# A two-layer decoder on one core: the opening of the first attention reordered, batch by batch, and the expert weights loaded in pieces

## The chip, the cores and the metric

One core of one Trainium2 chip runs the kernel. The metric is the device time of one execution in microseconds (us): the median of three timed runs, 528.86 before the change. A profile of one further execution goes with it.

## What is computed

Two decoder layers on x of 4 batches x 256 tokens x 128 features, all in float32, each with self attention, cross attention and a mixture of experts, always added to x after a layer norm. What the change touches is the first sublayer and the preparation of the second:

```python
q, k = rope(xn @ wq.T), rope(xn @ wk.T)        # 16 heads of 8 features
out  = softmax(q k^T / sqrt(8)) @ (xn @ wv.T)  # no mask, per batch of 256 tokens
# second sublayer, from the context alone:
K, V = ctx @ Wk.T, ctx @ Wv.T
ek   = exp(K - max over the 4 batches)         # keys
ep   = exp(W_bias - W_bias)                    # the maximum runs over an axis of length 1
num, den = ep @ (ek * V), ep @ ek
# third sublayer, 8 linear experts: each w_in[e] is multiplied with w_out[e] once
```

The rotated q and k are used as a rounded part and its rest (float32r, the one-pass matmul type), so that two one-pass products stand for one four-pass product.

## The kernel before, in words

The order of the work on each engine is written out by hand: one program per engine, which waits on named semaphores. Each engine runs its instructions in order, so a wait holds all that stands behind it. The 1024 tokens are 8 tiles of 128; a batch is 2 tiles, a half is 2 batches.

*Loads.* SP's queue (L259 to L287) issues 28 loads, x first, the 2 MB `wi0` and the 2 MB `wo0` of the experts last. ScalarE's queue (L461 to L463) issues the context `ctxT`, its weights `wctx`, then `ident`, the identity for transposes.

*Opening, TensorE* (L1160 to L1177): `context` (L1144), tiles 0 to 3, each giving keys and values of the second sublayer and values of the fifth, in banks 4 and 5 in turn, released by ScalarE's three copies (L475 to L477); `transpose_xn` of both halves (L1141); `rotary_projections(0)`, four 512-column products (q, k, and each with neighbours swapped; L1158); values of both halves (L1172); `context` tiles 4 to 7; `rotary_projections(1)`, each after VectorE's rotation has read the bank.

*Opening, the others.* VectorE: norm statistics, normalising, the rounding of the selection matrices `selr` (L752), the rotations of half 0 and the products of half 1 (`rotate`, L760, 512 wide), sums (L767) and rests (L772) of half 0, then the context's maximum over batches (L786 to L788). GpSimd: memsets (L323 to L335, three of them for later layers), `rstds` (L337), the sums of half 1 (L356), the context's differences (L360), the bias's difference (L364), the rests of half 1 (L368), then `head_values` (L344), which lays the values of four heads into `vaug`. ScalarE: copies, the rounded parts (L501), and the exponentials of context keys and bias (L516, L518).

*Attention* (`attention` on each engine, `pipelined`, L239): 4 batches of 16 slots plus a drain; slot k of batch b begins head k of batch b. The operands of a batch are *stacked* first: with `selr`, four heads' q and k (rounded part, rest) are put into one 128-row block `qk`, 32 rows per head. `first_stacks` (L1187) does this for batch 0, ScalarE copies the four groups out (L482); later batches are stacked inside the slots (`KEY_SLOTS`, `QUERY_SLOTS`) through bank 6. SP copies each head's 32 key rows into the zeroed `km` (`padded_keys`, L289 to L301: 4 copies of 32 KB per group of four heads). In slot k, `max_scores` (L1215) computes the scores whose row maxima VectorE takes (L823); in batch 0 it uses the stacked keys for groups 0 and 1 and `km` for 2 and 3. Every four heads the maxima are transposed into `qk` (L1259, L830). Seven slots later `exp_scores` (L1233) computes the scores again, with `km` and the maxima, and ScalarE takes the exponential (L541). Twelve slots after a group began come its values (L1262). The banks: 0 and 1 maxima, 2 and 3 exponentials, 4 values, 5 transposes, 6 stacks, 7 output rows.

The exponentials of the context are used by `aft_sums` (L1324) in the drain and after it. The expert weights are used at L1358, after the second sublayer.

Of the kernel before, what the change touches and what calls it, by code (L numbers as in the profile page):

```python
# [12 lines left out]
P = 128  # L13
# [10 lines left out]
FIRST_BANKS = (6, 7, 4, 5)  # L24
LN_EPS, Z_EPS = 1e-5, 1e-6
# [29 lines left out]
def decoder_kernel(nc, w, out):  # L55
# [4 lines left out]
    with ctx:  # L60
# [57 lines left out]
        ek = sb_early("ek", [P, TPB, B, D])  # L118
        ekv = sb_early("ekv", [P, TPB, B, D])
        v_tok = sb_early("v_tok", [P, NT, D])  # L120
        early.close()
# [22 lines left out]

# [3 lines left out]
        ctx_max = big[:, 6144:6912].rearrange("p (m k d) -> p m k d", m=3, k=TPB)  # L148
# [108 lines left out]
        def _(sp):  # L257
# [7 lines left out]
            load("xa0", wx0[:, :, :], w["wx0"])  # L265
            load("xa0", wbiasT[:, :, :], w["wbiasT"])
            load("gate0", wgate0[:, :], w["wgate0"])
            load("gate0", tie0[:, :, :], w["tie0"].partition_broadcast(P))
# [17 lines left out]
            load("ff0", wi0[:, :, :, :], w["wi0"])  # L286
            load("ff0", wo0[:, :, :, :], w["wo0"])  # L287

            def padded_keys(L):  # L289

                for n in range(B * G):
# [28 lines left out]
        def _(pool):  # L320
# [14 lines left out]
            pool.memset(first_row[0:1, :], 1.0).then_inc(s("at1_row"), 1)  # L335
# [15 lines left out]
            for hf in range(2):  # L351
                rstds("at0", hf)

            for n, a in enumerate((1, 0)):
                pool.wait_ge(s("at0_rot"), 4 + 2 * (n + 1))
                pool.tensor_tensor(rot1[1][:, a, :], rot1[1][:, a, :], rot2[1][:, a, :], ALU.add).then_inc(s("at0_sum1"), 1)  # L356

            pool.wait_ge(s("ctx_mx"), 1)
            for k in range(TPB):
                pool.tensor_tensor(ek[:, k, :, :], ek[:, k, :, :],  # L360
                                   ctx_max[:, 2, k:k + 1, :].broadcast_to([P, B, D]), ALU.subtract).then_inc(s("ctx_kd"), 1)

            pool.wait_ge(s("ld_xa0"), 32)
            pool.tensor_tensor(expbT[:, :, :], wbiasT[:, :, :], wbiasT[:, :, :], ALU.subtract).then_inc(s("ctx_kd"), 1)  # L364

            for n, a in enumerate((1, 0)):
                pool.wait_ge(s("at0_hi"), 2 + n + 1)
                pool.tensor_tensor(qlo[:, a, HALF:2 * HALF], rot1[1][:, a, :], qhi[:, a, HALF:2 * HALF].bitcast(f32),  # L368
                                   ALU.subtract).then_inc(s("at0_lo1"), 1)
            pool.wait_ge(s("at0_vev"), 2)  # L370
# [5 lines left out]
            pool.tensor_tensor(ekv[:, :, :, :], ek[:, :, :, :], ekv[:, :, :, :], ALU.mult).then_inc(s("ctx_ekv"), 1)  # L376
# [77 lines left out]
        def _(act):  # L454
# [6 lines left out]
            for name, dst, src in (("ctx", ctxT[:, :], "ctxT"), ("ctx", wctx[:, :, :], "wctx"),  # L461
                                   ("ident", ident[:, :], "ident")):
# [7 lines left out]
            def context(tiles):  # L470

                for n in tiles:
                    b, jt = n // TPB, n % TPB
                    act.wait_ge(s("ctx_pe"), n + 1)
                    act.activation(ek[:, jt, b, :], ps[:, 4 + n % 2, 0:D], ACT.Copy)  # L475
                    act.activation(ekv[:, jt, b, :], ps[:, 4 + n % 2, D:2 * D], ACT.Copy)
                    act.activation(v1_tok[:, n, :], ps[:, 4 + n % 2, 2 * D:3 * D], ACT.Copy).then_inc(s("ctx_ev"), 1)  # L477
# [19 lines left out]
            def rotated(hf):  # L497

                for n, a in enumerate((1, 0)):
                    act.wait_ge(s(("at0_sum", "at0_sum1")[hf]), n + 1)  # L500
                    act.activation(qhi[:, a, hf * HALF:hf * HALF + HALF], rot1[hf][:, a, :], ACT.Copy  # L501
                                   ).then_inc(s("at0_hi"), 1)

            context(range(NT // 2))
            for hf in range(2):
                evacuate_xnT("at0", hf)
            for hf in range(2):
                act.wait_ge(s("at0_v"), hf + 1)
                act.activation(v_tok[:, 4 * hf:4 * hf + 4, :], ps[:, 6 + hf, :].rearrange("p (n d) -> p n d", d=D),
                               ACT.Copy).then_inc(s("at0_vev"), 1)  # L510
            rotated(0)
            context(range(NT // 2, NT))
# [1183 lines left out]
```

## Time and profile before

| | |
|---|---|
| runs shown | 527.92, 528.86, 533.05 us; median 528.86 |
| profiled execution | 533.33 us, its span 531.6 us |
| mean granted TensorE clock | 0.931 of 2.4 GHz |
| busy: TensorE, VectorE, ScalarE, GpSimd | 87%, 66%, 61%, 25% of the span |
| the chain that ended last | TensorE 64%, VectorE 15%, "issue" 9%, ScalarE 6%, GpSimd 3%, DMA 2% |
| DMA | 16.07 MB, mean 30 GB/s; 8.82 MB of it in the first 30 us |

The chain is followed back from the last instruction: at each step to what released it. Shares are averages over stages with different limits. The first scores begin at 32.3 us. TensorE's busy time counts pipelined matmuls with modelled ends. Names in the rows: `bigr<-qk` on SP's queue are the padded keys, `nmax` VectorE's row maxima.

### The profile page before, as it was taken

The page shows a single profiled execution, that of the slowest core. Times are in us where ns is not written, and L with a number is a line of the kernel's source. Part 1 is how long each engine was busy: PE and PEld are TensorE (multiplying, and loading weights), DVE is VectorE, ACT ScalarE, POOL GpSimd, SP SyncE. Part 2 cuts the span into 40 slices and gives each one's busy share as a digit, 9 for nine tenths or more (in the row PEclk, how much of TensorE's full clock was granted, in tenths as well). Part 3 has the DMA queues.
Part 4 walks back from the last instruction along what each step waited for, and adds up shares of the span by engine and source line. Part 5 has one row for each costly group of instructions (what it writes and reads, how often), then busy time and mean ns, then how long its engine had stood idle before and what let it go on. Part 6 is the DMA issues. An engine that isn't in the chain of part 4 may idle for free.

```text
span 531.6 us, 8533 instructions
## 1 busy us (share of the span) xinstructions
PE 463.6 (87%) x2692; PEld 356.8 (67%) x2692; DVE 351.8 (66%) x967; ACT 324.8 (61%) x632; POOL 133.0 (25%) x195
## 2 busy tenths in 40 slices
PE   3777999988993998579999867999999999999995
PEld 2446777755831686448777745878778787878783
DVE  4375677767589565546778845858585767777653
ACT  2444767642255442035665527898988989898892
POOL 7060000212165100114545420121112221111121
PEclk9976999998998898857999977999999999999999
DMA  8911111000300000001111000000000000000001
GB/s 296 368 25 31 31 32 28 19 1 1 159 1 0 1 1 1 0 21 40 32 31 28 14 0 1 1 2 0 1 0 0 0 0 0 0 0 1 2 0 39
DMA packets 12754, 16.07 MB, mean 30 GB/s; under 512 B 4008, under 2 KB 11304, under 8 KB 12080
## 3 DMA queue, kind: packets, MB, share of 16 engines
q1 hardware_dynamic: 12288, 14.79, 8.8%
q10 hardware_dynamic: 432, 0.85, 0.4%
q8 instruction: 18, 0.29, 0.2%
q14 instruction: 16, 0.13, 0.1%
HBM read 10.92 MB, written 0.52 MB: 22 GB/s over the span
## 4 chain that ended last, share of the span: by engine, by line
PE 64%; DVE 15%; issue 9%; ACT 6%; POOL 3%; DMA 2%; SPq 1%; ACTq 0%; POOLq 0%; DVEq 0%
PE ps L1229 6%; PE ps L1274 4%; PE ps L1544 4%; PE ps L1545 4%; PE ps L1543 4%; PE ps L1562 4%; PE ps L1561 4%; PE ps L1560 4%; PE ps L1241 3%; POOL xnT L447 2%; DVE masked L816 2%; PE ps L1551 2%; PE ps L1462 2%; PE ps L1149 2%; DVE big L933 1%
## 5 line engine op out<-in xcount | busy, mean ns | idle before, releaser
L1078 DVE TENSOR_TENSOR bigr<-ps,bigr 128x512 fp32r<-128x512 f32 x128 | 86.3, 689 | 57.8 <-ACT ps L681 57.8
L541 ACT ACTIVATE big<-ps 128x512 f32<-128x512 f32 (+1 forms) x128 | 68.7, 548 | 52.9 <-PE ps L1241 50.9
L680 ACT ACTIVATE bigr<-ps,b 128x512 fp32r<-128x512 f32 x128 | 89.8, 702 | 3.6 <-PE ps L1545 0.7
L681 ACT ACTIVATE ps<-ps,b 128x512 f32<-128x512 f32 x128 | 86.6, 677 | 0.0
L447 POOL TENSOR_TENSOR xnT<-xnT,big 128x512 f32<-128x512 f32 x32 | 41.4, 1293 | 162.4 <-DVE big L1085 162.4
L1229 PE MATMUL ps<-bigr,qk 128*128 128x256 f32 (+1 forms) x224 | 53.8, 323 | 5.4 <-DMA bigr<-qk 2.8
L823 DVE TENSOR_REDUCE nmax<-ps 128x2 f32<-128x512 f32 x64 | 42.6, 688 | 18.8 <-PE ps L1229 18.4
L1241 PE MATMUL ps<-qk,bigr 128*128 128x256 f32 (+1 forms) x256 | 51.2, 284 | 1.0 <-ACT big L541 0.7
L1543 PE MATMUL ps<-k1hi,w1hi 128*128 128x512 f32 x128 | 51.5, 402 | 0.0
L1544 PE MATMUL ps<-k1hi,w1lo 128*128 128x512 f32 x128 | 51.3, 401 | 0.0
L1545 PE MATMUL ps<-k1lo,w1hi 128*128 128x512 f32 x128 | 51.2, 400 | 0.0
L1560 PE MATMUL ps<-bigr,w2hi 128*128 128x512 f32 x128 | 51.0, 398 | 0.0
L1562 PE MATMUL ps<-bigr,w2hi 128*128 128x512 f32 x128 | 50.7, 396 | 0.0
L1561 PE MATMUL ps<-bigr,w2lo 128*128 128x512 f32 x128 | 50.4, 394 | 0.0
L816 DVE CUSTOM_DVE_ANT_0 masked<-ps,later 128x128 f32<-128x128 f32 (+1 forms) x128 | 39.0, 352 | 16.2 <-PE ps L1229 15.8
L1229 PEld LDWEIGHTS ps<-bigr,qk 128*128 128x128 f32 x224 | 35.7, 200 | 14.6 <-issue 5.7
L1241 PEld LDWEIGHTS ps<-qk,bigr 128*128 128x128 f32 x256 | 41.2, 199 | 3.7 <-ACT big L541 2.3
L424 POOL TENSOR_SCALAR_AFFINE_SELECT big<-big 128x256 f32<-128x256 f32 x64 | 26.0, 411 | 46.5 <-ACT big L541 46.2
L1274 PE MATMUL ps<-big,vaug 128*32 128x256 f32 (+1 forms) x512 | 30.9, 358 | 2.2 <-POOL big L424 1.3
L672 ACT ACTIVATE big<-ps 128x512 f32<-128x512 f32 x32 | 19.2, 599 | 20.7 <-PE ps L1551 20.6
L1544 PEld LDWEIGHTS ps<-k1hi,w1lo 128*128 128x128 f32 x128 | 24.6, 192 | 6.0
L1545 PEld LDWEIGHTS ps<-k1lo,w1hi 128*128 128x128 f32 x128 | 24.5, 191 | 5.9
(200 smaller groups left out, 864.3 us busy)
## 6 DMA issues: line engine op xcount, KB each, us to landing
bigr<-qk SPq DMA_DIRECT2D x128, 32.0 KB, 1.9
wi<-in_wi SPq DMA_DIRECT2D x1, 2048.0 KB, 7.6
wo<-in_wo SPq DMA_DIRECT2D x1, 2048.0 KB, 12.1
big<-in_sel SPq DMA_DIRECT2D x1, 1024.0 KB, 8.6
wo<-in_w SPq DMA_DIRECT2D x1, 1024.0 KB, 4.8
wi<-in_w SPq DMA_DIRECT2D x1, 1024.0 KB, 6.9
x<-in_x SPq DMA_DIRECT2D x1, 512.0 KB, 5.5
ctxT<-in_ctxT ACTq DMA_DIRECT2D x1, 512.0 KB, 4.9
```

What stands on the lines that cost most here:

```text
L541: act.activation(prob[:, h % 8, c], ps[:, 2 + h % 2, c], ACT.Exp, scale=DH ** -0.5).then_inc(s(L + "_exp"), 1)
L680: act.activation(ghi[:, u % 2, c, :], ps[:, c, :], ACT.Gelu_apprx_tanh, bias=b1[:, u % E1, c:c + 1])
L681: act.activation(ps[:, c, :], ps[:, c, :], ACT.Gelu_apprx_tanh, bias=b1[:, u % E1, c:c + 1]).then_inc(s("ff1_gel"), 1)
L1078: v.tensor_tensor(glo[:, u % 2, c, :], ps[:, c, :], ghi[:, u % 2, c, :].bitcast(f32), ALU.subtract).then_inc(s("ff1_glo"), 1)
L1229: last = pe.matmul(ps[:, h % 2, at:at + seen], qk[rows, g, 0, t * P:t * P + P], keys[:, 0:seen], start=True, stop=True)
L1241: last = pe.matmul(ps[:, 2 + h % 2, at + first:at + T], km[:, h, t * P:t * P + P], qk[:, h // HPG, 0, first:T], start=True, stop=True)
L1543: pe.matmul(ps[:, k, :], w1hi[:, e, f], xhi[:, c], start=True, stop=False)
L1544: pe.matmul(ps[:, k, :], w1lo[:, e, f], xhi[:, c], start=False, stop=False)
L1545: pe.matmul(ps[:, k, :], w1hi[:, e, f], xlo[:, c], start=False, stop=True).then_inc(s("ff1_up"), 1)
L1560: pe.matmul(o, w2hi[:, e, k, :], ghi[:, u % 2, k, :], start=(k == 0), stop=False)
L1561: pe.matmul(o, w2lo[:, e, k, :], ghi[:, u % 2, k, :], start=False, stop=False)
L1562: last = pe.matmul(o, w2hi[:, e, k, :], glo[:, u % 2, k, :], start=False, stop=(k == FC - 1))
```

## The change

- *ScalarE's loads*: `ident` first, then `ctxT`, `wctx`.
- *TensorE ahead of the first stack*: context tiles 0 and 1, transposes of half 0, context tile 2, the four projections of half 0, transposes of half 1, context tile 3, values of half 0. VectorE rotates batch 0 (256 wide), sums and rests it, and multiplies batch 1, whose sum and rest go to GpSimd.
- *Inside batch 0's slots*: the projections of half 1 (into banks 2, 3, 7, 2), copied out raw by ScalarE, rotated and summed by GpSimd; values of half 1 and context tiles 4 to 7 (bank 7). Keys and values of a context tile are copied out in one ScalarE instruction instead of two.
- *Row maxima of batch 0* use the stacked keys for all four groups (in both attentions that share the code).
- *Context*: one VectorE reduction over the batches in slot 6 of batch 1; differences on GpSimd between its value copies; the exponentials in slots 3 and 14 of batch 2.
- *Expert weights*: instead of two loads of 2 MB in the opening, eight of 512 KB, one after each group's key copies in batches 1 and 2.
- `selr` is rounded by GpSimd; the three memsets for later layers come after the context products. Semaphores of loads and memsets are merged (`l0`, `zeroed`).

```diff
+            def expert_weights(part):
+                e = slice(2 * (part // 2), 2 * (part // 2) + 2)
+                dst, src = ((wi0, "wi0"), (wo0, "wo0"))[part % 2]
+                load("ff0", dst[:, e, :, :], w[src][:, e, :, :])
...
+                    between(n)
 
             sp.wait_ge(s("const"), 6)
-            padded_keys("at0")
+            padded_keys("at0", lambda n: expert_weights(n - G) if G <= n < G + E0 else None)
...
-            pool.memset(cwT[:, :, :].bitcast(f32), 0.0).then_inc(s("ff1_zero"), 1)
-            pool.memset(sel_er[:, :, :].bitcast(f32), 0.0).then_inc(s("ff1_zero"), 1)
-            pool.memset(first_row[:, :], 0.0).then_inc(s("at1_row"), 1)
-            pool.wait_ge(s("at1_row"), 1)
...
+            pool.wait_ge(s("ld_sel"), 32)
+            pool.tensor_copy(selr[:, :, :, :, :], sel).then_inc(s("sel_r"), 1)
 
...
+                pool.tensor_tensor(rot1[0][:, a, T:2 * T], rot1[0][:, a, T:2 * T], rot2[0][:, a, T:2 * T], ALU.add
+                                   ).then_inc(s("at0_sum1"), 1)
             for n, a in enumerate((1, 0)):
                 pool.wait_ge(s("at0_hi"), 2 + n + 1)
+                pool.tensor_tensor(qlo[:, a, T:2 * T], rot1[0][:, a, T:2 * T], qhi[:, a, T:2 * T].bitcast(f32),
+                                   ALU.subtract).then_inc(s("at0_lo1"), 1)
...
+            pool.wait_ge(s("at0_vev"), 1)
+            for g in range(G):
+                head_values("at0", v_tok, 0, g)
+
+            pool.wait_ge(s("ld_rope"), 16)
+            for n, a in enumerate((1, 0)):
+                for part, rows in enumerate((rot1[1], rot2[1])):
+                    pool.wait_ge(s("at0_raw"), 2 * n + part + 1)
+                    halves = rows[:, a, :].rearrange("p (b t) -> p b t", b=2)
+                    own.mark(pool.tensor_tensor(halves, halves, rope[:, part:part + 1, :].broadcast_to([P, 2, T]),
+                                                ALU.mult))
+                own.wait()
+                pool.tensor_tensor(rot1[1][:, a, :], rot1[1][:, a, :], rot2[1][:, a, :], ALU.add).then_inc(s("at0_sum1"), 1)
+            for n, a in enumerate((1, 0)):
+                pool.wait_ge(s("at0_hi"), 4 + n + 1)
                 pool.tensor_tensor(qlo[:, a, HALF:2 * HALF], rot1[1][:, a, :], qhi[:, a, HALF:2 * HALF].bitcast(f32),
...
-            for b in range(B):
+            for b in range(1, B):
                 for g in range(G):
                     head_values("at0", v_tok, b, g)
+                    if b == 1 and g >= G - TPB:
+                        context_differences(g - (G - TPB))
+                    if b == 2 and g == 0:
+                        pool.wait_ge(s("ld_l0"), 64)
+                        pool.tensor_tensor(expbT[:, :, :], wbiasT[:, :, :], wbiasT[:, :, :], ALU.subtract
+                                           ).then_inc(s("ctx_kd"), 1)
...
+            pool.memset(cwT[:, :, :].bitcast(f32), 0.0).then_inc(s("zeroed"), 1)
...
+            for name, dst, src in (("ident", ident[:, :], "ident"), ("ctx", ctxT[:, :], "ctxT"),
+                                   ("ctx", wctx[:, :, :], "wctx")):
...
+            def context(n, bank):
+                b, jt = n // TPB, n % TPB
+                act.wait_ge(s("ctx_pe"), n + 1)
+                act.activation(ek_ekv[:, :, jt, b, :], ps[:, bank, 0:2 * D].rearrange("p (a d) -> p a d", a=2), ACT.Copy)
+                act.activation(v1_tok[:, n, :], ps[:, bank, 2 * D:3 * D], ACT.Copy).then_inc(s("ctx_ev"), 1)
+
+            def self_values(hf, bank):
...
+            def raw_projection(n):
+                k = (2, 3, 0, 1)[n]
+                act.wait_ge(s("at0_qk"), 4 + n + 1)
+                act.activation((rot1[1], rot2[1])[k % 2][:, k // 2, :], ps[:, LATE_BANKS[n], :], ACT.Copy
+                               ).then_inc(s("at0_raw"), 1)
+
+            def rotated(ready, a, cols, source):
+                act.wait_ge(*ready)
+                act.activation(qhi[:, a, cols], source, ACT.Copy).then_inc(s("at0_hi"), 1)
 
...
+            context(0, 4)
+            context(1, 5)
+            evacuate_xnT("at0", 0)
+            context(2, 4)
+            rotated((s("at0_sum"), 1), 1, slice(0, T), rot1[0][:, 1, 0:T])
+            evacuate_xnT("at0", 1)
+            rotated((s("at0_sum"), 2), 0, slice(0, T), rot1[0][:, 0, 0:T])
+            context(3, 5)
+            self_values(0, 4)
+            evacuate_first_stacks("at0")
+            for n, a in enumerate((1, 0)):
+                rotated((s("at0_sum1"), n + 1), a, slice(T, 2 * T), rot1[0][:, a, T:2 * T])
...
+            def rotated_late():
...
+                    rotated((s("at0_sum1"), 2 + n + 1), a, slice(HALF, 2 * HALF), rot1[1][:, a, :])
+
+            def late_values():
+                self_values(1, 7)
+                act.wait_ge(s("at0_lo1"), 2)
+
+            def context_keys():
+                act.wait_ge(s("ctx_kd"), TPB)
+                act.activation(ek, ek, ACT.Exp).then_inc(s("ctx_ek"), 1)
...
+            def context_bias():
+                act.wait_ge(s("ctx_kd"), TPB + 1)
+                act.activation(expbT[:, :, :], expbT[:, :, :], ACT.Exp).then_inc(s("ctx_ek"), 1)
...
+                    if not causal and b == 2 and k == 3:
+                        context_keys()
+                    if not causal and b == 2 and k == 14:
+                        context_bias()
...
+            attention("at0", False, {0: lambda: raw_projection(0), 1: lambda: raw_projection(1),
+                                     2: lambda: raw_projection(2), 4: lambda: raw_projection(3), 6: late_values,
+                                     9: lambda: context(4, 7), 11: lambda: context(5, 7), 12: rotated_late,
+                                     13: lambda: context(6, 7), 15: lambda: context(7, 7)})
...
-            dve.wait_ge(s("ld_sel"), 32)
-            own.mark(v.tensor_copy(selr[:, :, :, :, :], sel))
...
+            def rotate(b, a):
+
+                c = slice(b * T, b * T + T)
+                for part_, dst in enumerate((rot1[0], rot2[0])):
+                    dve.wait_ge(s("at0_qk"), 2 * (1 - a) + part_ + 1)
+                    v.tensor_tensor(dst[:, a, c], ps[:, 2 * a + part_, c], rope[:, part_, :], ALU.mult
                                     ).then_inc(s("at0_rot"), 1)
...
+            def context_maxima():
+                dve.wait_ge(s("ctx_ev"), NT)
+                v.tensor_reduce(ctx_max[:, :, :], ek.rearrange("p k b d -> p k d b"), AX.X, ALU.max
+                                ).then_inc(s("ctx_mx"), 1)
+
+            rotate(0, 1)
             rotated_sum(0, 1)
-            rotate(0, 1, 0)
+            rotate(0, 0)
             rotated_rest(0, 1)
             rotated_sum(1, 0)
-            rotate(1, 0, 1)
+            rotate(1, 1)
             rotated_rest(1, 0)
-            rotate(1, 1, 0)
...
+                    if b == 1 and not causal and k == 6:
+                        context_maxima()
...
+            context(0, 4)
+            context(1, 5)
...
-            for hf in range(2):
...
+            transpose_xn("at0", 0)
+            pe.wait_ge(s("ctx_ev"), 1)
+            context(2, 4)
             pe.wait_ge(s("ld_w0"), 16)
             pe.wait_ge(s("ln_xnT"), ln("at0", 2) + 1)
-            rotary_projections(0)
...
+            for n, k in enumerate((2, 3, 0, 1)):
+                rotary_projection(0, n, k)
+            transpose_xn("at0", 1)
+            pe.wait_ge(s("ctx_ev"), 2)
+            context(3, 5)
+            pe.wait_ge(s("ctx_ev"), 3)
+            self_values(0, 4)
...
-                    if b == 0 and g < 2:
+                    if b == 0:
                         rows = slice(QUAD * (h % HPG), QUAD * (h % HPG) + QUAD)
                         keys = qk[rows, g, 1, :]
                         pe.wait_ge(s(L + "_stkev"), g + 1)
...
+            def late_projections(k):
+                if k == 0:
+                    rotary_projection(1, 0, LATE_BANKS[0])
+                elif k == 1:
+                    rotary_projection(1, 1, LATE_BANKS[1])
+                    pe.wait_ge(s("at0_stkev"), 2)
+                    rotary_projection(1, 2, LATE_BANKS[2])
+                elif k == 3:
+                    pe.wait_ge(s("at0_raw"), 1)
+                    rotary_projection(1, 3, LATE_BANKS[3])
+                elif k == 5:
+                    pe.wait_ge(s("at0_raw"), 3)
+                    self_values(1, 7)
+                elif k == 6:
+                    pe.wait_ge(s("at0_raw"), 4)
+
+            def late_context(n):
+                if n == 4:
+                    pe.wait_ge(s("at0_vev"), 2)
+                else:
+                    pe.wait_ge(s("ctx_ev"), n)
+                context(n, 7)
...
+            pe.wait_ge(s("sel_r"), 1)
+            pe.wait_ge(s("ln_xnT"), ln("at0", 2) + 2)
+            pe.wait_ge(s("at0_vev"), 1)
+            pe.wait_ge(s("ctx_ev"), NT // 2)
+            attention("at0", False, qhi[:, 1, :], qlo[:, 1, :],
+                      {0: (s("at0_lo"), 2), 1: (s("at0_lo1"), 2), 2: (s("at0_lo1"), 4)},
+                      lambda: pe.wait_ge(s("at0_rot"), 8), aft_sums,
+                      early={0: lambda: late_projections(0), 1: lambda: late_projections(1),
+                             3: lambda: late_projections(3), 5: lambda: late_projections(5),
+                             6: lambda: late_projections(6), 8: lambda: late_context(4), 10: lambda: late_context(5),
+                             12: lambda: late_context(6), 14: lambda: late_context(7)})
```

## Rows read from the trace of the kernel before

**Rows 1.** Chain of waits, 0 to 34 us: start us, us, what.
```profile
1.64 6.30 DMA wctx<-in_wctx
7.98 5.49 PE ps L1149 x8
13.47 0.79 PE ps L1141 x4
...
15.02 3.67 PE ps L1158 x8
18.69 1.80 PE ps L1172 x16
...
24.17 2.86 PE ps L1149 x4
27.03 3.83 PE ps L1158 x8
...
31.56 0.70 ACT qk L482
```

**Rows 2.** Busy time by stretch: stretch, length, engines (instructions), granted clock, DMA share, GB/s.
```profile
24.00:27.60 3.60, 3.43 (x5) 1.78 (x6) 0.00 (x0) 1.77 (x10) 0.00 (x0) 0.54 0.67 287
32.30:34.60 2.30, 0.59 (x4) 0.43 (x5) 2.27 (x4) 2.30 (x5) 1.48 (x2) 0.98 0.12 29
34.60:38.00 3.40, 3.10 (x10) 2.26 (x10) 2.70 (x5) 1.95 (x3) 3.40 (x4) 0.50 0.22 51
38.00:43.20 5.20, 2.41 (x10) 1.72 (x8) 1.99 (x4) 0.69 (x2) 2.60 (x6) 0.50 0.18 42
43.20:48.10 4.90, 4.88 (x23) 4.88 (x24) 2.71 (x5) 2.73 (x5) 0.00 (x0) 0.50 0.08 19
48.10:52.50 4.40, 4.07 (x39) 3.13 (x39) 3.38 (x6) 3.02 (x6) 0.24 (x1) 0.99 0.16 37
```

**Rows 3.** Chain of waits, 31 to 75 us: scores of heads 8, 16, 24, 32.
```profile
43.22 0.79 PE ps L1229 x2
...
52.68 0.24 PE ps L1229 x2
...
61.30 0.24 PE ps L1229 x2
...
70.33 0.36 PE ps L1229 x2
```

**Rows 4.** Instructions by shape, 0 to 50 us: busy us, mean ns, idle before.
```profile
L823 DVE TENSOR_REDUCE nmax<-ps 128x2 f32<-128x512 f32 x13 | 8.6, 689 | 5.9 <-PE ps L1229 5.9
...
L541 ACT ACTIVATE big<-ps 128x512 f32<-128x512 f32 x6 | 3.5, 596 | 6.9 <-PE ps L1241 6.8
...
L356 POOL TENSOR_TENSOR xn<-xn,big 128x512 f32<-128x512 f32 x2 | 3.0, 1520 | 18.9 <-DVE big L760 18.8
...
L360 POOL TENSOR_TENSOR ek<-ek,big 128x512 f32<-128x512 f32 x2 | 2.5, 1268 | 0.8 <-DVE big L788 0.8
...
L787 DVE TENSOR_TENSOR big<-ek 128x256 f32<-128x256 f32 x1 | 1.5, 1495 | 0.0
...
L516 ACT ACTIVATE ek<-ek 128x1024 f32<-128x1024 f32 x1 | 1.1, 1057 | 1.5 <-POOL ek L360 1.5
```

**Rows 5.** DMA issues (KB each, median us to landing), then issues in order of time.
```profile
bigr<-qk SPq DMA_DIRECT2D x128, 32.0 KB, 1.9
...
big<-in_sel SPq DMA_DIRECT2D x1, 1024.0 KB, 8.6
wo<-in_w SPq DMA_DIRECT2D x1, 1024.0 KB, 4.8
...
ident<-in_ident ACTq DMA_DIRECT2D x1, 64.0 KB, 7.6
...
2.12 0.45 ACTq L463 DMA_DIRECT2D ident<-in_ident  x1
...
57.00 1.23 SPq L300 DMA_DIRECT2D bigr<-qk  x2
```

More of the change, by code:

```diff
@@ L24 @@
 FIRST_BANKS = (6, 7, 4, 5)
+LATE_BANKS = (2, 3, 7, 2)
 LN_EPS, Z_EPS = 1e-5, 1e-6
@@ L468, in evacuate_xnT @@
                                ).then_inc(s("ln_xnT"), 1)
[L470 to L477, printed above, removed]
+            def context(n, bank):
[4 more added lines that the diff above has]
+            def self_values(hf, bank):
+                act.wait_ge(s("at0_v"), hf + 1)
+                act.activation(v_tok[:, 4 * hf:4 * hf + 4, :], ps[:, bank, :].rearrange("p (n d) -> p n d", d=D),
+                               ACT.Copy).then_inc(s("at0_vev"), 1)
+            def raw_projection(n):
[6 more added lines that the diff above has]
+                act.activation(qhi[:, a, cols], source, ACT.Copy).then_inc(s("at0_hi"), 1)
             def evacuate_first_stacks(L):
@@ L507, in _ @@
[L507 to L512, printed above, removed]
-            evacuate_first_stacks("at0")
-            rotated(1)
-            act.wait_ge(s("ctx_kd"), TPB)
-            act.activation(ek[:, :, :, :], ek[:, :, :, :], ACT.Exp).then_inc(s("ctx_ek"), 1)
@@ L708, in _ @@
             gelus(0, 0)
-            act.wait_ge(s("ff1_zero"), 2)
+            act.wait_ge(s("zeroed"), 2)
             gate_rows(0, 0, 6)
@@ L1142, in transpose_xn, with context @@
                 last.then_inc(s("ln_xT"), 1)
[L1144 to L1158 removed]
+            def context(n, bank):
+                pe.matmul(ps[:, bank, 0:3 * D], ctxT[:, n * P:n * P + P], wctx[:, 0:3, :], start=True, stop=True
+                          ).then_inc(s("ctx_pe"), 1)
@@ new lines, in rotary_projection, with self_values @@
+            def rotary_projection(hf, n, bank):
+                pe.matmul(ps[:, bank, :], w0[:, (2, 3, 0, 1)[n], :], xnT[:, hf * HALF:hf * HALF + HALF],
+                          start=True, stop=True).then_inc(s("at0_qk"), 1)
+            def self_values(hf, bank):
+                for n in range(4):
+                    tile = 4 * hf + n
+                    last = pe.matmul(ps[:, bank, n * D:n * D + D], xnT[:, tile * P:tile * P + P], w0[:, 4, :],
+                                     start=True, stop=True)
+                last.then_inc(s("at0_v"), 1)
@@ L1160, in _ @@
             pe.wait_ge(s("ld_ctx"), 32)
-            context(range(NT // 2))
+            context(0, 4)
+            context(1, 5)
             pe.wait_ge(s("ld_ident"), 16)
-            for hf in range(2):
-                transpose_xn("at0", hf)
+            transpose_xn("at0", 0)
+            pe.wait_ge(s("ctx_ev"), 1)
+            context(2, 4)
             pe.wait_ge(s("ld_w0"), 16)
             pe.wait_ge(s("ln_xnT"), ln("at0", 2) + 1)
-            rotary_projections(0)
-            for hf in range(2):
-                pe.wait_ge(s("ln_xnT"), ln("at0", 2) + hf + 1)
-                for n in range(4):
-                    tile = 4 * hf + n
-                    last = pe.matmul(ps[:, 6 + hf, n * D:n * D + D], xnT[:, tile * P:tile * P + P], w0[:, 4, :],
-                                     start=True, stop=True)
-                last.then_inc(s("at0_v"), 1)
@@ L1176, in _, with attention @@
-            context(range(NT // 2, NT))
-            rotary_projections(1)
-            def attention(L, causal, k_hi, k_lo, half_ready, before_first, aft_sums=None, beside={}, early={}):
+            for n, k in enumerate((2, 3, 0, 1)):
[5 more added lines that the diff above has]
+            self_values(0, 4)
+            def attention(L, causal, k_hi, k_lo, batch_ready, before_first, aft_sums=None, beside={}, early={}):
```

101 lines of the change are left out of this document (31 added, 70 removed).

## The prediction

> **What bounds the kernel now.** I read four views. First the chain of waits over the opening [rows 1]: the reader is to see that nothing but TensorE work on *all* 1024 tokens stands ahead of the first softmax head. TensorE starts at 7.98, when the context weights have landed, does the first four context tiles, turns, projects and stacks, and the first stacked block is copied out only at 31.56. Second the busy time by stretch [rows 2]: the granted clock is at its low level (1.2 GHz, half) in 24.0 to 27.6, after TensorE's values had ended at 20.5 and its next context tiles had waited until 24.17 for ScalarE [rows 1], and again in 34.6 to 48.1, after TensorE had been busy 0.59 of 2.30 us; it is back in 48.1 to 52.5, after TensorE was busy 4.88 of 4.90. So the opening pays twice: for order, and for a clock lost by gaps. Third the chain of the first attention batch [rows 3]: the heads of group 2 wait until 43.22 for their padded keys. The first batch's 16 slots run from about 32.3 to 52.7 (20.4 us), the second's from 52.68 to 70.33 (17.65 us). Fourth, durations by shape and the DMA issues [rows 4, 5], for the prices.
>
> My yardstick is the start of the second batch's first scores: 52.68 before. What follows it is in steady state and shifts with it.
>
> **Part 1: ahead of the first stack.** Landing: ident is now issued ahead of the context's two loads on ScalarE's queue, so the weights that start TensorE are third instead of second. Ends: 7.98 as now, and 9.7, where the third load of that queue (ident, issued at 2.12, 7.6 us to landing [rows 5]) lands today. 64 KB more of 832 KB would say 8.4; I take 8.9, the middle, since the row for a third load is nearer in kind than a count of bytes. The Trainium skill, DMA: Bandwidth & Descriptors, section Queues, rings and completion order, says that each DMA engine goes round the queues packet by packet; by that the last load of the queue would land when the queue's three are through, at 9.7, and the total would be 0.8 us higher. No row here separates the two.
>
> Then, at the rates of [rows 1]: two context tiles at 1.28 us (8 instructions in 5.49 us with short waits; two per tile) to 11.5; four transposes, 0.79, to 12.3; the third context tile, 1.28, to 13.6, beside which ScalarE copies the turned tokens. Four projections of 512 columns: 3.67 us for eight instructions with the clock high; I add 0.3 for a start with it low: 17.5. Four transposes, one context tile and four value tiles (half of 1.80) with the clock high: 0.4 + 0.64 + 0.9, to 19.4. VectorE's rotations are halved in width and run beside this; the last value copy (0.6, as a 512-wide ScalarE copy [rows 4]) ends at about 20.1. Stacking takes as long as now (0.75): the first copy starts at about 20.9 instead of 31.56, **10.7 us earlier**. What left the path: a second set of four projections (3.83), four context tiles with their waits, four value tiles.
>
> At nothing I cost: the rounding of the selection matrices, moved to GpSimd. It may start when its load lands (8.6 us after an issue next to ident's, so about 11 [rows 5]) and is needed at 20; bounds 1.3 and 5.1 us (one and four times GpSimd's 512-wide two-input operation, 1.27, for 2048 columns [rows 4]); both end before 16.5. Three memsets go behind the context products on GpSimd, which then waits for the next layer's statistics anyway; nothing before the later layers needs them. SP's queue loses two issues in the opening, behind all that the opening needs. VectorE's context maximum leaves the path of its first reductions.
>
> **Part 2: the first batch.** It takes in what was removed: four projections, four value tiles, four context tiles on TensorE, 3.7 + 0.9 + 2.6 = 7.2 us with the clock high; on ScalarE four raw copies, one value copy, four context copies and two rotated halves, eleven of about 0.6 us [rows 4]; on GpSimd four multiplications and two sums (6 x 1.27 to 1.52 = 7.6 to 9.1 us [rows 4]) and two differences. It loses the wait for padded keys: all 16 heads now take their row maxima from the stacked keys, and the padded keys are wanted first at slot 7, about 9 us after the copies begin, where a group's four issues take some 2.5 us (two take 1.23) and landing 1.9 [rows 5].
>
> Slots 0 to 6: eight score pairs at 0.24 [rows 3], four projections at 0.92 (a quarter of 3.67), values 0.9, a transposed maximum 0.2, and 0.6 of waits for the reductions (0.69 each [rows 4]): 7.3 us from 21.7 (copy and start as now), with the clock high. But TensorE is busy only 0.75 us between 19.4 and 21.7, a gap like the ones before 24.0 and 34.6, so I expect one more low stretch, taken at 4.5 us, between the two of [rows 2] in which TensorE was busy throughout (3.6 and 4.9 us); half of it is lost, +2.2. Slot 7 begins at 31.2. From there ScalarE sets the pace: nine exponentials at 0.5, four contexts at 0.6, two rotated halves 1.2, keys and queries 1.3, 0.6 of values: 10 us. The second batch starts at about 41.2 instead of 52.7: **11.5 us earlier**, bounds 14.6 (no fall, early landing) and 5.7 (rival C).
>
> **Part 3: what later batches take in.** VectorE's context maximum, 1024 elements in one reduction, at slot 6 of batch 1: 1.3 us (twice 0.69), against two buffers of scores; cost 0 to 1.3, I take 0.5. The exponential of the context keys on ScalarE (1.06 [rows 4]) at slot 3 of batch 2: 0 to 1.1, I take 0.5; that of the bias, half as wide: 0.2. These were free in the stall; in steady state TensorE is over 90% busy (4.07 of 4.40 [rows 2]) and little hides them wholly. The expert weights come in eight pieces of 512 KB, each behind a group's four key copies on SP's queue, in batches 1 and 2. Price: 0, since the last copy for group 2 is issued at 57.6 [rows 5], lands 1.9 later and is used at 61.30 [rows 3], a margin of 1.8 us, and a piece is issued over a microsecond ahead of the next group. Upper bound under D. They are used only after the attention, long after batch 2.
>
> **Sum.** -10.7 to the first copy, -0.8 more over the first batch, +1.2 later: **-10.3 us**. The profiled execution took 533.33 (span 531.6); it is 0.8% above the median of the runs shown, 528.86. So 523.0 on its own scale, and **518.6** on that of the median, which I give.
>
> **The rivals.**
> A, forecast (0.55): as above, 515.5 to 522.
> B (0.15): the clock does not fall in the first batch, the landing stays at 8.0, later pieces hide: -10.3 - 2.2 - 0.9 - 1.2 = -14.6, 514.3. For it: with the stack in it the gap is shorter than that before 24.17. Against: the clock was low right after the stretch with 0.59 of 2.30 us busy.
> C (0.17): the clock stays low through most of the first batch, because TensorE waits for ScalarE's copies between late projections and context tiles. Slots 0 to 8 hold some 8 us of work with the clock high; all of it at half costs 8 instead of 2.2: -4.5, 524.4. For it: low from 34.6 to 48.1 before, with stretches 91% and 46% busy [rows 2]. Against: dense work brought it back.
> D, slower (0.06): the expert pieces hold up the key copies behind them. Place: SP's queue in batches 1 and 2, eight groups. Price if a key copy waits for a piece's whole landing, bounded by the 1024 KB weight load on a quiet queue (4.8 us [rows 5]): 8 x (4.8 - 1.8) = +24, hence 542.6. It decides against the change from 1.8 + (10.3 + 5.3)/8 = 3.8 us of delay per group on. Against: of the 4.8 us, 1.9 is what even a 32 KB copy takes; half of the other 2.9, for half the bytes, is 1.5 us of transfer, less than the margin. The Trainium skill, the same page and section, says that within a queue each DMA engine takes descriptors in order; by it the copies would stand behind a piece for what is left of its transfer, which the margin covers. The rows show key copies only on a quiet queue.
> E (0.07), the gain is not there, since the stall only moves: GpSimd's rotations are late and ScalarE, in order, waits for them at slot 12, holding the exponentials. At 1.52 each, begun at 25.5 after the first batch's own pieces, the six end near 34.6, and ScalarE gets there near 36; if each of the eight is held up as VectorE's 256-wide maximum was beside GpSimd (1.50 us, 0.8 more than a reduction twice as wide [rows 4]), 6.5 us are added: -3.8, 525.1. Against: the first batch's thirteen reductions, half of them beside GpSimd's operations, kept a mean of 0.69.
>
> **How the numbers follow.** About 1% (5.3 us) is what a measurement of this kernel can tell from none. Faster by more: A, B and a third of C, 0.76. Within: the rest of C and nearly all of E, 0.17. Slower: D and a tail of E, 0.07. Range 513 to 526: A, B and C, with D, E and tails left out.
>
> **What would show it.** First copy of the stacked block near 21 (wrong if past 25: then part 1 failed). Scores of head 8 not waiting for a DMA. Clock low for one stretch after the first stack and high by slot 8; if it is low until 40, C. Second batch's first scores near 41. No wait of the scores for padded keys in batches 1 and 2; if there is one in each of eight groups, D. ScalarE waiting for GpSimd's sums at slot 12 would be E. The span behind the second batch as long as before but for about 1.2 us; more would make the forecast wrong in a part I hold unchanged.

## The result and the profile after

The changed kernel took 532.4 us in the median of 20 runs (529.19 to 538.56), the kernel before 529.25 beside it (527.69 to 533.17, 20 runs): a ratio of 1.0057, 95% interval [1.0033, 1.0082] (two runs in a slower state, 538.20 and 538.56, are not in the ratio). The forecast was 518.6 with 513 to 526, so the time fell outside the range on the far side of no change. The profiled execution took 534.82 (span 533.1, mean granted clock 0.925; before: span 531.6, 0.931).

The chain of waits of the kernel after over its opening and first batch (start us, us, what) answers to [rows 1] and [rows 3].

```profile
2.15 7.78 DMA wctx<-in_wctx
...
9.97 2.93 PE ps L1197 x4
...
14.27 3.69 PE ps L1202 x8
...
22.30 0.47 PE ps L1279 x2
...
33.87 0.44 PE ps L1279 x2
34.30 0.43 PE ps L1291 x2
...
39.38 0.43 PE ps L1279 x2
39.81 0.43 PE ps L1291 x2
...
46.09 0.24 PE ps L1279 x2
46.33 0.24 PE ps L1291 x2
```

L1197 is the context product, L1202 a projection, L1279 the scores for the row maxima, L1291 those for the exponentials. The opening came out much as drawn: the first copy of the stacked block starts at 21.51 (before 31.56, forecast 20.9). But the second batch begins at 46.09, not 41.2: 6.6 us of the 11.5 are there. The lines at 33.87 and 39.38 show why: in slots 7 to 15 each pair of a maximum and an exponential costs 0.87, with the same instruction counts that cost 0.48 (0.24 and 0.24) at 46.09, in the second batch.

The stretches of the same kernel (stretch and length, then busy us of PE, weight loads, DVE, ACT, POOL with instructions, granted clock, DMA share, GB/s) answer to [rows 2].

```profile
23.50:30.00 6.50, 6.50 (x12) 2.68 (x12) 1.39 (x4) 2.72 (x6) 5.61 (x9) 0.50 0.24 56
...
33.10:38.00 4.90, 4.90 (x26) 3.50 (x26) 3.65 (x6) 3.29 (x8) 1.06 (x1) 1.00 0.03 8
38.00:45.90 7.90, 7.90 (x48) 4.65 (x47) 3.60 (x6) 5.14 (x14) 2.69 (x3) 1.00 0.31 88
```

The clock is at its high level in all of 33.1 to 45.9, so 0.87 a pair is not a clock price. And TensorE is busy for 7.90 of 7.90 us while ScalarE has 5.14: TensorE sets the pace there, not ScalarE.

Its weight loads say where the time is (timeline of TensorE's loads: start, us, line, operation, tile, count):

```profile
38.45 0.29 PEld L1279 LDWEIGHTS ps<-qk 32*128 32x128 f32 x2 [0.55 <-issue]
38.87 0.30 PEld L1291 LDWEIGHTS ps<-qk,bigr 128*128 128x128 f32 x2
39.31 0.29 PEld L1279 LDWEIGHTS ps<-qk 32*128 32x128 f32 x2
39.74 0.30 PEld L1291 LDWEIGHTS ps<-qk,bigr 128*128 128x128 f32 x2
...
45.81 0.31 PEld L1279 LDWEIGHTS ps<-bigr,qk 128*128 128x128 f32 x2
46.05 0.31 PEld L1291 LDWEIGHTS ps<-qk,bigr 128*128 128x128 f32 x2
```

The maxima load 32 rows of the array (a head's own stacked keys), the exponentials all 128 (the padded ones), in turns. Each load of the next form starts only as the last matmul of the other ends (39.31 and 39.74 stand 0.07 ahead of the matmuls of 39.38 and 39.81), so it isn't taken in beside them. In the second batch, where every load has 128 rows, the loads of 45.81 and 46.05 stand 0.28 ahead of their matmuls (46.09 and 46.33 in the chain), beside the matmuls before them. The Trainium skill, TensorE: Matmul & The Clock Gate, in Part 3, section The mechanism, says that a load is pulled ahead of matmuls in flight when it goes to rows that don't conflict, or to a second, background weight buffer. The first agrees with the 0.07: a 128-row load conflicts with every 32-row strip. It would not explain the 0.28, where the rows are the same; why the second doesn't help when the form changes, no row shows.

Up to the end of the self-attention the lead shrinks to 5.0 us: the next layer's sums begin at 101.53 (L1381) against 106.53 (L1331) before. The rest goes in the cross attention of the second layer, which runs the same code. There the new condition had no wait to take away: in the kernel before, no score of its first batch waits for a padded key. By the first copy of its stacked block the lead had grown to 7.65 (224.53 against 232.18), in layers that the change leaves alone; just ahead of it the granted clock was 0.89 (195 to 224.5) against 0.79 (200 to 232.1). Then, the chain before and after over that attention's first batch:

```profile
232.18 0.70 ACT qk L482
...
242.19 0.44 PE ps L1229 x2
242.63 0.32 PE ps L1241 x2
...
246.97 0.79 PE ps L1274 x16
...
254.73 0.79 PE ps L1274 x16
```
```profile
224.53 0.69 ACT qk L523
...
234.55 0.72 PE ps L1279 x2
235.27 0.62 PE ps L1291 x2
...
242.76 1.44 PE ps L1324 x16
...
249.73 0.43 PE ps L1279 x2
...
255.10 0.79 PE ps L1324 x16
```

At the third set of values (254.73 and 255.10) the lead of 7.65 is a lag of 0.37. In these slots a pair of a maximum and an exponential costs 1.34 against 0.76, and the low clock is in both. The stretches after, and below them those before:

```profile
228.00:246.00 18.00, 18.00 (x70) 11.82 (x69) 9.45 (x55) 5.73 (x11) 4.07 (x9) 0.50 0.14 32
246.00:251.50 5.50, 5.50 (x26) 4.37 (x30) 2.35 (x13) 2.47 (x6) 1.65 (x5) 0.50 0.10 24
251.50:254.00 2.50, 2.50 (x31) 2.03 (x24) 1.23 (x8) 1.29 (x4) 0.57 (x2) 0.89 0.00 0
```
```profile
228.00:246.00 18.00, 15.10 (x66) 10.46 (x65) 10.24 (x54) 6.87 (x13) 1.74 (x6) 0.50 0.12 29
246.00:251.50 5.50, 5.26 (x56) 4.40 (x59) 3.93 (x25) 3.74 (x9) 3.82 (x9) 0.99 0.17 40
```

After, TensorE counts as busy for every microsecond of 228 to 251.5 and yet stays at 1.2 GHz; before, it left that level near 246. From the last values of that attention (304.2 and 303.7) to the end the two kernels differ by 1.0 us more (228.8 against 227.8, at a clock of 0.95 and 0.97).

### The profile page after: what moved, and what is told of

It reads as the page before. It is cut to its first block, busy times and chain, and to the rows that moved or that the text cites. A ratio compares the mean times of both kernels' runs of the same rounds, so it can differ in the third digit from the quotient of the medians.

```text
span 533.1 us, 8560 instructions
## 1 busy us (share of the span) xinstructions
PE 469.8 (88%) x2692; PEld 355.5 (67%) x2692; DVE 347.6 (65%) x964; ACT 327.1 (61%) x630; POOL 142.6 (27%) x204
## 4 chain that ended last, share of the span: by engine, by line
PE 65%; DVE 16%; issue 9%; ACT 5%; POOL 3%; DMA 1%; ACTq 0%; POOLq 0%; DVEq 0%
PE ps L1279 7%; PE ps L1324 5%; PE ps L1624 4%; PE ps L1625 4%; PE ps L1623 4%; PE ps L1642 4%; PE ps L1641 4%; PE ps L1640 4%; PE ps L1291 4%; DVE masked L868 2%; POOL xnT L476 2%; PE ps L1202 2%; PE ps L1631 2%; PE ps L1542 2%; DVE big L985 1%
## 5 line engine op out<-in xcount | busy, mean ns | idle before, releaser
L875 DVE TENSOR_REDUCE nmax<-ps 128x2 f32<-128x512 f32 x64 | 42.8, 689 | 24.8 <-PE ps L1279 24.3
L1291 PE MATMUL ps<-qk,bigr 128*128 128x256 f32 (+1 forms) x256 | 53.2, 293 | 1.0 <-ACT big L592 0.7
L1279 PE MATMUL ps<-bigr,qk 128*128 128x256 f32 (+1 forms) x192 | 45.0, 316 | 4.1 <-DVE nmax L875 2.6
L1291 PEld LDWEIGHTS ps<-qk,bigr 128*128 128x128 f32 x256 | 41.0, 199 | 6.5 <-ACT big L592 2.5
L1279 PEld LDWEIGHTS ps<-bigr,qk 128*128 128x128 f32 x192 | 29.1, 190 | 12.9 <-issue 7.0
L1324 PE MATMUL ps<-big,vaug 128*32 128x256 f32 (+1 forms) x512 | 32.7, 375 | 2.2 <-POOL big L453 1.3
```

Of the source, the lines that this page charges most:

```text
L1279: last = pe.matmul(ps[:, h % 2, at:at + seen], qk[rows, g, 0, t * P:t * P + P], keys[:, 0:seen], start=True, stop=True)
L1291: last = pe.matmul(ps[:, 2 + h % 2, at + first:at + T], km[:, h, t * P:t * P + P], qk[:, h // HPG, 0, first:T], start=True, stop=True)
```

## The experiments

The suspect is one line that both attentions share, the condition under which a head of the first batch takes its maxima from the 32 stacked rows. I call the theory F (the 32-row form of groups 2 and 3 costs it) and the rival P (chance: the long low stretch in the cross attention comes from where the earlier start falls in time, whatever the form).

Each ratio below is to the kernel before, run beside that experiment: 531.91 us beside e1 to e4, 528.98 beside e5 to e8, 529.05 beside e10. So ratios compare across these groups, and times don't.

**The condition undone in both attentions** (e1_g2_both), and **the condition alone, put on the kernel before** (e2_before_b0, the same edit the other way round):

```diff
-                    if b == 0:
+                    if b == 0 and g < 2:
```

> The changed kernel with one line back: in batch 0 of both attentions, heads of groups 2 and 3 take their row maxima from the padded keys (128 rows) as before the change. Theory F (form): a slot that mixes 32-row and 128-row scores costs 0.86 instead of 0.48 us with the clock high, and holds the clock low in the cross attention's first batch. Then the self attention gains about 8 x 0.38 = 3 us and the cross attention about 8 us: 521 (518 to 525), and the clock in the cross attention returns some 8 us earlier. Rival P (chance): the long low stretch of the clock in the cross attention comes from where the earlier start falls, whatever the form: then only the 3 us come, 529.5. Padded keys of group 2 land near 32 and are wanted near 34, so no wait for them by either.

> The kernel before with that one line of the change alone: all four groups' row maxima of batch 0 from the stacked keys (32 rows). Theory F: the wait for padded keys in the self attention goes (-3), its slots 8 to 15 cost the same at the low clock and the clock comes back later (+2 to +4), and the cross attention loses about 8: 536 (533 to 540), slower than before. Rival P: without the earlier start the cross attention is as before and the 3 us of waiting are gained: 526.

Measured: 524.94 us, 0.9899 [0.9838, 0.9959] of before; and 542.12, 1.0243 [1.0171, 1.0316]. Both on F's side, the second by more than I gave it. So the line alone makes the old kernel slower and its removal makes the new one faster than the old. In the second run the clock was low from 33.8, behind the first four score matmuls (31.88), to 57.7 in the self-attention (before: up to 48.1 [rows 2]) and up to 262.5 in the cross attention (before 246.1).

**The condition undone in one attention** (the cross attention in e3_g2_cross, the self-attention in e4_g2_self):

```diff
-                    if b == 0:
+                    if b == 0 and (g < 2 or not causal):    # e3
+                    if b == 0 and (g < 2 or causal):        # e4
```

In this code the flag named causal is false for the self-attention.

> The changed kernel with the padded keys back for groups 2 and 3 of the cross attention alone. Theory F: -8 us, 524 (521 to 527), with the clock back by the ninth slot of the cross attention. Rival P: no change, 532.

> The changed kernel with the padded keys back for groups 2 and 3 of the self attention alone. Theory F: slots 8 to 15 of its first batch at 0.48 per pair of scores instead of 0.86, 3 us less: 529.5 (528 to 531); the second batch starts near 43 instead of 45.9; the cross attention stays slow. Rival P: the same by the form; but if the gain of the other run is larger than the sum of the two single ones, the two are not separate.

Measured: 525.21, 0.9898 [0.9862, 0.9934]; and 532.84, 1.0032 [1.0000, 1.0065]. The cross attention has nearly the whole loss; what the self-attention's edit gives back (1.0057 to 1.0032, some 1.3 us) is too little to tell, since the two intervals overlap. What the form costs in the self-attention by itself is seen between e1 and e3, whose clock is high all through that batch: the second values (L1324) begin at 42.41 and at 45.13, 2.7 us apart, of which 0.7 is the later stack of e3 (its first product at 21.84, in e1 at 21.17) and 2.0 the form. By 99.01 and 100.02, where the next layer's sums begin, 1.0 is left of the 2.7.

**Switch or size?** Is a 32-row matmul dear, or the change from one form to the other? In e5_pairs slots 7 to 14 are paired, two heads' maxima and then two heads' exponentials, which halves the changes:

```diff
+                    if b == 0 and 7 <= k <= 14:
+                        if k % 2:
+                            max_scores(0, k).then_inc(s(L + "_mx"), 1)
+                            max_scores(0, k + 1).then_inc(s(L + "_mx"), 1)
+                            exp_scores(0, k - 7).then_inc(s(L + "_s"), 1)
+                            exp_scores(0, k - 6).then_inc(s(L + "_s"), 1)
+                        return
```

> The changed kernel, in batch 0 of both attentions the scores of slots 7 to 14 in pairs: both maxima's scores (32 rows), then both exponentials' scores (128 rows), so half as many changes between the two forms with the same matmuls. Theory S (switch): the extra 0.38 us of a slot is the weight load that TensorE does not take ahead across a change of form; half the changes save half of it: 8 x 0.19 = 1.5 us in the self attention and some 8 x 0.3 = 2.4 us in the cross attention at the low clock: 528.5 (526 to 530.5). Rival R (rows): a 32-row matmul is slow in itself, with whatever stands beside it: 532.4 as the changed kernel, pairs of scores still at 0.86.

Measured: 533.3, 1.0069 [1.0031, 1.0108]. The time gives R its number, but not its reason. TensorE's timeline in e5, at the high clock (start, us, what, in brackets the wait ahead):

```profile
34.16 0.47 PE L1279 MATMUL ps<-qk 32*128 32x256 f32 x2 [0.76 <-DVE nmax L875]
...
38.41 0.91 PE L1197 MATMUL ps<-wctx,ctxT 128*128 128x384 f32 x2 [0.44 <-ACT v_tok L503]
39.26 0.51 PE L1279 MATMUL ps<-qk 32*128 32x256 f32 x4
39.69 0.74 PE L1291 MATMUL ps<-qk,bigr 128*128 128x256 f32 x4
40.36 1.07 PE L1331 MATMUL ps<-big,vaug 128*32 128x256 f32 x16
```

Starts tell it (the ends of merged rows overlap): four 32-row matmuls take 0.43, from 39.26 to 39.69, as long as two in the kernel after. Four 128-row matmuls take 0.67, from 39.69 to 40.36: 0.43 as in the kernel after, and the second pair the 0.24 that a pair costs behind its own form. Two heads go from 39.26 to 40.36: 0.55 a head against 0.87, near the 0.48 of the 128-row form. So the switch is the price, and a run of 32-row matmuls isn't dear. (Two heads' keys stand in different strips of the array, so their matmuls may also have run side by side; no run here separates that from a load taken in ahead.) But the new order makes TensorE wait for VectorE and ScalarE (0.76, and 0.44 twice, 1.6 us in all), and the waits eat what the pairing saves: by the chain it takes 13.0 us from slot 7 to the second batch (33.30 to 46.29), against 12.9 (33.19 to 46.09). In the cross attention the clock again stayed low, to 255.6.

**The load order** (e6_load_order: ident behind the context's loads again) and **the pieces** (e7_no_pieces: the expert weights as two 2 MB loads in the opening again):

```diff
-            for name, dst, src in (("ident", ident[:, :], "ident"), ("ctx", ctxT[:, :], "ctxT"),
-                                   ("ctx", wctx[:, :, :], "wctx")):
+            for name, dst, src in (("ctx", ctxT[:, :], "ctxT"), ("ctx", wctx[:, :, :], "wctx"),
+                                   ("ident", ident[:, :], "ident")):
```
```diff
+            load("ff0", wi0[:, :, :, :], w["wi0"])
+            load("ff0", wo0[:, :, :, :], w["wo0"])
...
-            padded_keys("at0", lambda n: expert_weights(n - G) if G <= n < G + E0 else None)
+            padded_keys("at0")
...
```

> The changed kernel with the loads of ScalarE's queue in the old order: context, its weights, ident. If the first step of the forecast failed by the third place in the queue, TensorE starts near 8.0 instead of 9.97 and the first stack comes 1 to 2 us earlier (ident, third, then lands near 9.7, ahead of the transposes near 11); the end of the first attention moves by as much, unless a low stretch of the clock falls otherwise: 530.9 (529.5 to 532.4). If the opening is bound by something else (the normalised tokens, VectorE), no change: 532.4.

> The changed kernel with the expert weights in the opening again, two loads of 2 MB at the end of SP's queue, none among the key copies. By the forecast the pieces cost nothing: 532.4 (531.5 to 533.5). Rival D (the pieces hold up the key copies): faster by 3 us or more, and the scores of batches 1 and 2 wait less for key copies. A third way: the 4 MB, at the engines until about 27, hold up the first key copies near 22: the exponentials' first scores wait, up to 2 us slower.

Measured: 528.89, 0.9994 [0.9957, 1.0030]; and 532.29, 1.0064 [1.0023, 1.0104]. The old load order is worth about 0.6% of the time, some 3 us, a little more than expected; the two intervals just miss each other. TensorE starts at 8.11 instead of 9.97, which explains 1.9. What else it gives isn't shown: a clock that falls or not in the first batch moves the next layer's sums by as much from one profiled execution to another (by TensorE's timeline 101.53 in the kernel after, 99.61 in e7, 99.86 in e3, with one load order and one self-attention condition in all three). The pieces cost and give nothing, so D had no part in it.

**What the experiments point to** (e8_combined: the condition undone in both, the old load order, and the context maximum as two reductions in slots 3 and 7):

> Three edits on the changed kernel together: padded keys back for groups 2 and 3 in both attentions; the old load order; the context's maximum in two reductions of half the size, in slots 3 and 7 of batch 1, instead of one of 1.9 us in slot 6. Against the first of these alone (0.9899 of before): -1.5 for the load order and -0.5 to -1 for the maximum: 0.986 of before, 522 (519.5 to 525). If ScalarE or the key copies set the pace of the first batch by then, the load order gives nothing: 0.9899.

Measured: 522.52, 0.9864 [0.9798, 0.9930], as expected; against e1 (0.9899) the intervals overlap.

**The clock in the cross attention** (e10_g1_cross: e8, with group 1 of that attention's first batch on padded keys as well):

```diff
-                    if b == 0 and g < 2:
+                    if b == 0 and g < (1 if causal else 2):
```

> e8_combined with one more group of the cross attention's first batch (group 1, heads 4 to 7) taking its row maxima from the padded keys. Its time was 522.5, and TensorE's clock in the cross attention came back at 234. Theory K, the 32-row score matmuls are what TensorE runs while the clock stays low, and it comes back soon after the last of them: the clock comes back 2 to 4 us earlier, near 231, and the time falls by about half of that, 521. Rival T, the clock comes back some time after the stack whatever form the scores have: back at 234 again, 522.5. Rival L, the padded keys of group 1 are not there yet at slot 4 and TensorE waits for the copies: 2 to 3 us lost, 525.

Measured: 518.3, 0.9799 [0.9767, 0.9832], the lowest ratio here and more than K gave it (521), though its interval overlaps that of e8. TensorE does wait for the copies, as L said, but that isn't what decides. Its timeline and stretches in e10, and then the stretches of e8:

```profile
219.22 1.32 PE L1279 MATMUL ps<-qk 32*128 32x128 f32 x4 [0.76 <-DVE nmax L868]
...
223.87 1.22 PE L1279 MATMUL ps<-bigr,qk 128*128 128x128 f32 x4 [2.29 <-DMA bigr<-qk]
...
226.00:228.00 2.00, 2.00 (x8) 1.32 (x7) 0.55 (x4) 0.60 (x1) 0.00 (x0) 0.56 0.21 49
228.00:230.00 2.00, 1.84 (x14) 1.47 (x13) 2.00 (x12) 1.33 (x3) 0.69 (x2) 1.00 0.07 16
```
```profile
230.00:232.00 2.00, 2.00 (x12) 2.00 (x11) 1.97 (x13) 1.37 (x3) 0.88 (x3) 0.50 0.15 35
232.00:234.00 2.00, 2.00 (x13) 2.00 (x11) 1.36 (x8) 1.25 (x3) 0.85 (x3) 0.54 0.00 0
```

The clock is back at 227.7 instead of 233.8. Of these 6.1 us, 2.8 are an earlier start: the stack of this attention begins at 215.6 in e10 and at 218.5 in e8, behind code that the two share. Counted from the stack, the clock returns 3.3 us earlier, with 2.29 us of waiting on the way, and from the stack to the end e10 takes 0.8 us less (300.2 against 300.9). So K has its earlier clock and T is out, but most of the distance between these two profiled executions (3.6 us of span) lies ahead of the edit.

The same reading of all eleven traces, in the cross attention's first batch: how many of the four groups take their maxima from 32 rows, where the stack's first product starts, the start of the last 32-row score, where the granted clock comes back (us of the span), and three distances:

| kernel | 32-row groups | stack | last 32-row score | clock back | from last score | from stack | stack to end |
|---|---|---|---|---|---|---|---|
| before | 2 | 230.9 | 240.5 | 246.1 | 5.6 | 15.2 | 300.7 |
| after | 4 | 223.3 | 248.1 | 252.0 | 3.9 | 28.7 | 309.8 |
| e1 | 2 | 220.3 | 229.9 | 236.0 | 6.1 | 15.7 | 301.1 |
| e2 | 4 | 233.1 | 257.9 | 262.5 | 4.6 | 29.4 | 307.2 |
| e3 | 2 | 222.1 | 231.7 | 237.6 | 5.9 | 15.5 | 301.0 |
| e4 | 4 | 221.4 | 246.2 | 250.7 | 4.5 | 29.3 | 307.1 |
| e5 | 4 | 225.7 | 248.9 | 255.6 | 6.7 | 29.8 | 308.1 |
| e6 | 4 | 221.5 | 246.3 | 250.9 | 4.6 | 29.4 | 307.2 |
| e7 | 4 | 221.8 | 246.6 | 251.0 | 4.4 | 29.2 | 306.8 |
| e8 | 2 | 218.5 | 228.1 | 233.8 | 5.7 | 15.4 | 300.9 |
| e10 | 1 | 215.6 | 220.0 | 227.7 | 7.7 | 12.1 | 300.2 |

The number of 32-row groups sorts the last two columns without an exception, wherever the stack falls in time, and P would have it otherwise: with four groups the clock comes back some 14 us later than with two, and 6 to 9 us are lost from there to the end. In none of them did the clock come back while 32-row scores were still to come. It isn't a law of the form: in the self-attention of the kernel after, the clock came back at 30 with 32-row maxima before and behind it, where projections of 512 columns lay between them and no exponentials yet. What TensorE must run for the clock to return was not measured further.

## Why the prediction was wrong, step by step

**The steps that failed: the yardstick's "What follows it is in steady state and shifts with it", and part 2's price of the score pairs.** The larger one is the yardstick. The code is shared, as the description of the change says, but I sized it for the self-attention alone and put the second user of the line at nothing, without a reason. The sign that I had named for this came: from the second batch's first scores to the end of the span the kernel after takes 487.0 us (46.09 to 533.1) against 478.9 (52.68 to 531.6), 8.1 more where I had allowed 1.2. The cross attention's first batch turned a lead of 7.65 into a lag of 0.4, which e3 gives back (0.9898 against 1.0057 is 1.6%, 8.4 us). The trace of before had shown both its 32-row scores and the clock that returned only behind them, and the sum used neither.

In part 2 I priced a pair of matmuls at 0.24 from [rows 3], rows of padded keys, 128 rows of the array, and from slot 7 on gave TensorE's pairs no term at all, since ScalarE was to set the pace. The change moves groups 2 and 3 to 32 rows, in turns with 128-row exponentials: 0.43 and 0.43. Eight slots (8 to 15) at 0.39 more are 3.1 us on a stretch that I had at 10 us from slot 7; it took 12.9 (33.19 to 46.09). Inside those 10 us the exponentials stand at 0.5, where [rows 4] have 0.596: another 0.9 that the sum left out.

**Part 1** held in structure. TensorE started at 9.97, not 8.9: the third load of the queue landed at 9.93. That agrees with what I cited of the Trainium skill (DMA: Bandwidth & Descriptors, Queues, rings and completion order), by which it would be 9.7, and my middle value was the wrong choice. From there the first copy came 11.54 later (forecast 12.0).

**Part 2, slots 0 to 6.** One low stretch after the first stack, as forecast, but 6.8 us long (23.3 to 30.2) instead of 4.5; slot 7 at 33.2 instead of 31.2, with 0.6 of it from the later first copy. That it came in the execution shown was luck: of the nine traces with the new opening only after and e5 have it. In e3, whose self-attention is that of the kernel after, and in e1, e4, e6, e7, e8 and e10 the clock stayed at 1.00 through the same slots, so B's first condition came true in them. "From there ScalarE sets the pace" was wrong: TensorE did. The wait for padded keys is gone, as forecast, but in the self-attention it could have stayed gone without the condition: in e1 TensorE waits for a key copy once in that batch, for 0.2 us: group 2's copies land at 31.50, 8.9 us after the first was issued, while slots 0 to 7 run the work that was moved into them.

**Part 3.** The context maximum took more than twice a reduction of half its size (1.87 by the chain, 1.3 forecast) and did stall TensorE. The chain of the kernel after in batch 1:

```profile
52.91 0.33 DVE qk L882
53.23 1.87 DVE ctx_max L829
55.10 0.61 DVE nmax L875
...
55.84 0.47 PE ps L1279 x2
```

TensorE waited 1.12 us for the maximum behind it (L875). From the second batch to the next layer's sums the kernel after took 55.44 (46.09 to 101.53) against 53.85: 1.6 for the 1.2 forecast.

**The rivals.** D: each piece takes 4.5 us to land, but no score of batches 1 and 2 waits for a key copy, and e7 shows the same time without pieces. E: ScalarE doesn't wait for GpSimd's sums. C named the right symptom, a clock low through a first batch, in the wrong attention and for another reason. None of the five had the mechanism that decided.

**What could have been had.** With the condition undone, the load order restored and the maximum split, the rest of the change is worth 1.4% (e8), 7 us, where I had forecast 10.3 for the whole; with group 1 of the cross attention on padded keys too, 2.0% (e10). By the two profiled executions e8 is 12.2 us shorter than before (spans 519.4 and 531.6), since that of before ran 0.8% above its median and that of e8 0.3% below. My 10.3 came from that one execution, with the time that its clock cost; how much of it a median run loses, no trace here shows.

## What to carry to other kernels

Price a moved or widened instruction by a row of its own form and of its own neighbours: a pair of 32-row matmuls in turns with a pair of 128-row ones cost 0.43 and 0.43 us, against 0.24 for a 128-row pair among its own kind. When a diff touches a function that two stages call, walk through both stages, the later one first at the clock that it has there. And a wait that is removed may have been the cheaper side: in e10, 2.29 us of waiting for padded keys cost nothing by the end (300.2 us from the stack on, against 300.9 in e8, one profile each), and in the self-attention the wait was 0.2 us once the slots ahead of it were full. Last, a forecast from one profiled execution takes over that execution's clock: the same code gained or lost a low stretch of 6.8 us from one profile to the next.

## What the hardware showed that was not expected

At the high clock, four 32-row matmuls of 256 columns in a row took as long (0.43 us) as two that stood between 128-row ones, and a 128-row pair took 0.43 behind 32-row ones and 0.24 behind its own kind. TensorE could count as busy for 23.5 us on end (228 to 251.5) and stay at 1.2 GHz. And in the cross attention its return to 2.4 GHz followed the end of the 32-row scores in eleven traces of eleven, 3.9 to 7.7 us behind the last of them.
